# Routing in two batches, scaled expert results in a table read linearly, and the bias product last, in a graph layer with a 16-expert block on one Trainium2 core

## The chip, the cores and the metric

The kernel runs on one core of one Trainium2 chip. Its time is device microseconds for one launch, as the median of several runs. TensorE is called PE in the profile, VectorE DVE, ScalarE ACT, GpSimd POOL and SyncE SP.

## The reference

There are 1250 nodes of 512 features and 20000 edges with a source, a destination, one of 4 types and a weight. Everything is float32.

```
xn  = layernorm(x)
msg = sum over types r of (xn[src] @ W_rel[r] + b_rel[r]) * (weight where type == r)
agg = segment_sum(msg, dst) / max(segment_sum(weight, dst), 1)
x1  = layernorm(xn + xn @ W_self + b_self + agg) * g1 + b1
y   = layernorm(x1 + gelu(x1 @ W_ffn1 + b_ffn1) @ W_ffn2 + b_ffn2) * g2 + b2
x   = x + y
xm  = layernorm(x)
p   = softmax(xm @ router_w.T + router_b)            # 16 experts
out = x + sum over the two experts e with the largest p of
          p[e] * (gelu(xm @ w1[e].T + b1[e]) @ w2[e].T + b2[e])
```

## The kernel before, in words

The nodes are padded to 1280, ten tiles of 128 rows. All stages are in one program; the engines meet by semaphores, and the order of the work on each engine is the order in which `program` writes it down.

**Products.** PE turns each normed tile (`turn_xn`, L749, three tiles ahead of the products) and multiplies it with the four type matrices and with W_self (`product`, L756). DVE writes the low parts of the turned tiles (`x_low`, L1051), takes the products out and adds biases (L1130), and works out the tables of the edges (`edge_tables`, L1077) after the third product. SP stores the results as a table of messages.

**Gathers and the first half.** POOL gathers 157 chunks of 128 message rows with indirect DMAs (L522). PE sums them in windows (`window_sums`, L787). ACT copies each window sum twice, plain and rounded (`sums_out`, L605), DVE subtracts (`low_sums`, L1154), and PE adds the windows to blocks (`add_windows`, L799). Beside this, for pairs of tiles `p`, PE does the two-layer product (`hidden`, `second`), DVE the norm before it (`first_norm`) and the two after it (`other_norms`, L1205), and PE turns the normed tile (`turn_xm`) and makes its 16 logits (`logits`). Both products of the routing wait for the last pair. When the last window is summed, POOL clears a tile of zeros (L527), and SP fills `xslot` and the end of `yslot` with it (L425).

**Routing.** With all logits there, DVE adds the router's bias, ACT takes the exponential, and DVE finds for all ten tiles at once the two experts of every node, its gates, and the row that it gets in `xslot`, where each expert's rows are put together and rounded up to tiles of 128 (L1303 to L1347). POOL then writes every tile twice with 20 indirect DMAs (L543), one for the first and one for the second expert. Meanwhile DVE makes the table of which expert a slot tile has (L1349 to L1363), and PE multiplies the gates with the experts' second biases (L930 to L941), which DVE adds to `x_res` (L1367).

**Experts.** SP loads slot tiles, five ahead, and PE handles 28 of them in a fixed order. In step `t` it turns the rows of tile t+2 (`turn_rows`, L949), does the first product of t+1, the second product of t, and turns the hidden rows of t+1 (`expert_tiles`, L985). DVE copies the hidden rows (L1374) and the result (`take`, L1376). SP stores the result as soon as `take` is done and then loads tile t+5 into the place of tile t's rows (L440 to L452). POOL loads the next expert's weights, one megabyte, when a place of the five is free (L549 to L558).

**End.** When all results are stored, POOL gathers for each node tile the two result rows (L569, 20 indirect DMAs), DVE scales and adds them to `x_res` (L1407, L1410), and SP stores the tile (L468).

## Time and profile before

| what | value |
|---|---|
| median of 3 runs | 641.01 us (640.02 to 641.83) |
| profiled execution, its own time | 639.41 us |
| its span, first to last instruction | 637.5 us |
| mean granted clock of PE | 0.905 of full speed |
| PE, DVE, ACT, POOL busy | 526.0, 320.0, 119.3, 229.9 us |
| experts, from the first turn of slot rows to the last `take` | 467.0 to 597.6 us |

The busy times are sums over the whole span and overlap. PE is busy for 82% of the span, but not evenly: it is nearly full up to 407 us and in the expert loop, and has little or nothing to do between 407 and 467 us and after 597 us.

### The profile page before, as it was taken

The numbers are of one execution on the slowest core, as the hardware profiler recorded it, in microseconds if no ns is written. First come the engines' busy times: TensorE is split into PE (matmuls) and PEld (weight loads), VectorE is DVE, ScalarE is ACT, GpSimd is POOL, SyncE is SP. The second block draws the span as 40 slices with busy tenths as digits, with TensorE's granted clock in tenths as the row PEclk, the third lists the DMA queues.
The fourth block names the chain that finished last, engine by engine and source line by source line (L and its number), as shares of the span: only waits on it lengthen the run. The fifth ranks groups of instructions, "written<-read, shape, count | busy, mean of one in ns | idle before, by whom it ended". The sixth has DMA issues, their size and how long they took to land.

```text
span 637.5 us, 7136 instructions
## 1 busy us (share of the span) xinstructions
PE 526.0 (82%) x2292; PEld 353.1 (55%) x2292; DVE 320.0 (50%) x847; ACT 119.3 (19%) x251; POOL 229.9 (36%) x270
## 2 busy tenths in 40 slices
PE   1999999999965999999999999529359999999300
PEld 1888888887612756656657667223146666666200
DVE  6788563212226145986977995948102222222144
ACT  2121101000111322322223312011022222222000
POOL 3630000037777777777773000004700011110273
PEclk9999999989977999999999999855569999999855
DMA  8427242249898677776774592442534477872285
GB/s 318 185 83 255 113 166 92 90 121 290 278 398 283 195 203 201 200 199 178 200 204 123 201 407 86 155 178 99 207 105 165 164 265 265 293 267 100 85 257 203
DMA packets 47703, 125.54 MB, mean 197 GB/s; under 512 B 6496, under 2 KB 7136, under 8 KB 45360
## 3 DMA queue, kind: packets, MB, share of 16 engines
q0 software_dynamic: 17344, 63.20, 32.3%
q1 hardware_dynamic: 27360, 57.57, 24.1%
q10 hardware_dynamic: 2960, 4.27, 2.3%
q8 instruction: 22, 0.36, 0.2%
q14 instruction: 17, 0.14, 0.1%
HBM read 85.70 MB, written 39.32 MB: 196 GB/s over the span
## 4 chain that ended last, share of the span: by engine, by line
PE 74%; POOL 8%; DVE 7%; issue 5%; DMA 4%; ACT 1%; POOLq 1%; ACTq 0%; SPq 0%; DVEq 0%
PE ps L828 11%; PE ps L839 10%; PE ps L961 8%; PE ps L978 8%; PE ps L762 7%; PE ps L763 7%; PE ps L764 7%; PE ps L794 6%; POOL greg L569 3%; POOL xslot L543 3%; PE ps L954 2%; POOL greg L522 2%; PE ps L805 2%; PE ps L860 1%; DMA x_res<-x 1%
## 5 line engine op out<-in xcount | busy, mean ns | idle before, releaser
L522 POOL DMA_INDIRECT greg<-msg,row_i x157 | 156.7, 998 | 145.0 <-DMA msg<-greg 93.6
L762 PE MATMUL ps<-w_hi,xT_hi 128*128 128x512 f32 x200 | 81.1, 405 | 0.0
L763 PE MATMUL ps<-w_lo,xT_hi 128*128 128x512 f32 x200 | 79.8, 399 | 0.0
L764 PE MATMUL ps<-w_hi,xT_lo 128*128 128x512 f32 x200 | 79.7, 398 | 0.0
L828 PE MATMUL ps<-freg,wreg 128*128 128x256 f32 x320 | 71.7, 383 | 0.8 <-ACT freg L622 0.8
L839 PE MATMUL ps<-wreg,freg 128*128 128x512 f32 x160 | 72.1, 598 | 0.0
L828 PEld LDWEIGHTS ps<-freg,wreg 128*128 128x128 f32 x320 | 60.3, 191 | 16.4 <-issue 7.5
L961 PE MATMUL ps<-wreg,freg 128*128 x224 | 55.7, 393 | 0.0
L978 PE MATMUL ps<-wreg,freg 128*128 x112 | 52.7, 593 | 0.9 <-ACT freg L709 0.9
L794 PE MATMUL ps<-greg,sel 128*32 128x512 f32 x320 | 47.9, 638 | 6.3 <-DMA greg<-msg,row_i 6.3
L543 POOL DMA_INDIRECT xslot<-work,pos_i x20 | 19.7, 986 | 85.2 <-DVE pos_i L1347 79.4
L1374 DVE COPY freg<-ps 128x256 f32<-128x256 f32 x28 | 11.9, 425 | 74.8 <-PE ps L961 74.8
L839 PEld LDWEIGHTS ps<-wreg,freg 128*128 128x128 f32 x160 | 29.3, 190 | 35.4 <-issue 35.3
L1130 DVE TENSOR_TENSOR greg<-ps,greg 128x512 f32<-128x512 f32 x40 | 27.5, 688 | 36.0 <-PE ps L764 36.0
L961 PEld LDWEIGHTS ps<-wreg,freg 128*128 128x128 f32 x224 | 42.2, 199 | 5.5 <-issue 0.4
L762 PEld LDWEIGHTS ps<-w_hi,xT_hi 128*128 128x128 f32 x200 | 38.0, 190 | 10.5 <-issue 1.7
L764 PEld LDWEIGHTS ps<-w_hi,xT_lo 128*128 128x128 f32 x200 | 38.1, 191 | 9.5
L763 PEld LDWEIGHTS ps<-w_lo,xT_hi 128*128 128x128 f32 x200 | 38.2, 191 | 8.8
L1157 DVE TENSOR_TENSOR q_lo<-q_all,q_hi 128x512 fp32r<-128x512 f32 x20 | 13.9, 694 | 54.2 <-ACT q_hi L610 53.5
L1378 DVE COPY greg<-ps 128x512 f32<-128x512 f32 x28 | 19.4, 692 | 38.5 <-PE ps L978 38.5
L954 PE MATMUL ps<-ident,greg 128*128 128x128 f32 x112 | 18.3, 291 | 22.0 <-DMA greg<-xslot 14.7
L608 ACT COPY q_all<-ps 128x512 f32<-128x512 f32 x20 | 11.7, 586 | 119.9 <-PE ps L794 119.9
(170 smaller groups left out, 648.3 us busy)
## 6 DMA issues: line engine op xcount, KB each, us to landing
wreg<-experts POOLq DMA_DIRECT2D x11, 1025.0 KB, 6.3
msg<-greg SPq DMA_DIRECT2D x40, 256.0 KB, 2.0
xslot<-greg SPq DMA_DIRECT2D x1, 8960.0 KB, 25.6
greg<-xslot SPq DMA_DIRECT2D x28, 256.0 KB, 4.1
yslot<-greg SPq DMA_DIRECT2D x28, 256.0 KB, 2.9
wreg<-experts SPq DMA_DIRECT2D x5, 1025.0 KB, 9.6
wreg<-w SPq DMA_DIRECT2D x8, 512.0 KB, 12.7
w_in<-w_rel ACTq DMA_DIRECT2D x3, 1024.0 KB, 6.5
```

Source lines behind the costliest of these rows:

```text
L522: nc.gpsimd.indirect_dma_start(gath[:, c % RING, :], None, msg, bass.IndirectOffsetOnAxis(ap=row_i[:, c:c + 1], axis=0)).then_inc(s_gath[c ...
L543: nc.gpsimd.indirect_dma_start(xslot, bass.IndirectOffsetOnAxis(ap=pos_i[:, 2 * t + c:2 * t + c + 1], axis=0), work[:, t, :], None).then_i ...
L762: nc.tensor.matmul(bank(t % 5), xT_hi[:, at], w_hi[:, i, wk], start=(k == 0), stop=False)
L763: nc.tensor.matmul(bank(t % 5), xT_hi[:, at], w_lo[:, i, wk], start=False, stop=False)
L764: mm = nc.tensor.matmul(bank(t % 5), xT_lo[:, at], w_hi[:, i, wk], start=False, stop=(k == KD - 1))
L794: mm = nc.tensor.matmul(ps[WIN * j:WIN * (j + 1), B_Q * D:(B_Q + 1) * D], sel[:, c, :], gath[:, at % RING, :], start=(i == 0), stop=(i == ...
L828: mm = nc.tensor.matmul(bank(B_F1 + (f + 1) % 2, 0, 2 * P), w1_v[:, k, f * P:(f + 1) * P], x1T[:, k, :, :].rearrange("p s n -> p (s n)"), ...
L839: mm = nc.tensor.matmul(bank(B_F2), hT[:, f, s * P:(s + 1) * P], w2_v[:, f, :], start=(f == 0), stop=(f == KF - 1))
L954: tr = nc.tensor.transpose(bank(m, k * P, P), xs[:, u % MR, k * P:(k + 1) * P], ident[:, :])
L961: mm = nc.tensor.matmul(bank(3, 0, EF), xsT[:, SCR[u % MR], k, :], wreg[:, ds(at + k * EF, EF)], start=(k == 0), stop=(k == KD - 1))
L978: mm = nc.tensor.matmul(bank(5 + m), ehT[:, m, f, :], wreg[:, ds(at + (KD * EF + f * D), D)], start=(f == 0), stop=(f == KE - 1))
L1130: v.tensor_tensor(stage[:, n % 5, :], bank(t % 5), bias[:, V_REL + r, :], ALU.add).then_inc(s_evac, 1)
```

## The change

- The transposes of the first stage run two tiles ahead of the products, not three. The plain copy `q_all` is gone: DVE subtracts from PSUM itself. POOL adds the second norm's bias to `x_res` early, so `other_norms` has one DVE operation less.
- Routing is done in two batches, tiles 0 to 7 and tiles 8 and 9, by two new DVE functions, `choose` (experts) and `place` (rows). Batch 0's parts stand before and after the norms of tile 8, and POOL scatters its 16 times while DVE goes on. Batch 1's rows go into what is left of the tiles, or behind them, so the rows of a slot tile may lie in two stretches.
- Rows of `xslot` are 516 words wide: features, twice the node's number, its first expert, and its two gates. The slots are cleared after the last gather is issued; a second DMA then writes the number of each slot into one column.
- POOL loads each slot tile by an indirect gather, four ahead, and writes each result, scaled with its gate by DVE, with an indirect scatter to `results[2 * node + which]`. SP loads the experts' weights.
- At the end SP loads `results` linearly, a pair of tiles per DMA, and DVE adds without scaling. The product of gates and second biases is done after the expert loop.

The diff, cut to its core:

```diff
+BATCHES = ((0, NT - 2), (NT - 2, NT))
+AHEAD = 4
+BIAS_TILES = ((0, 4), (4, 8), (8, NT))
...
@@ SP @@
+            def clear_slots(before):
+                sp.dma_start(slots, empty_slots.unsqueeze(1).to_broadcast([P, SLOT_TILES, XW])).then_inc(s_zero, 16)
+                sp.wait_ge(s_zero, before + 16)
+                sp.dma_start(slots[:, :, C_ID:C_ID + 1], slot_ids.unsqueeze(2),
+                             allow_slow_non_contiguous=True).then_inc(s_zero, 16)
...
-            sp.wait_ge(d_sc, 16 * 2 * NT)
-            for u in range(MR):
-                load_x(u, u)
-            with sp.Fori(0, LOOPED - 1) as it:
-                for u in range(MR):
-                    store(it * MR + u, u)
-                    load_x(it * MR + (u + MR), u)
+            sp.wait_ge(d_tab, 1)
+            for e in range(EXPERTS):
+                if e >= MR:
+                    sp.wait_ge(e_y, done[e - MR])
+                    load_expert(sp, e)
+                sp.wait_ge(e_w[e % MR], 16 * (e // MR + 1))
+                sp.sem_inc(e_landed, 1)
+            results_out(0, USUAL)
+            for p in range(PAIRS):
+                sp.dma_start(both[:, 2 * p:2 * p + 2, :],
+                             results[4 * p * P:4 * (p + 1) * P, :].rearrange("(t p c) d -> p t (c d)", t=2, c=2))\
+                    .then_inc(f_in[p], 16)
@@ POOL @@
+            def scatter(r, b):
+                pool.wait_ge(r.pos, b + 1)
+                for t in range(*BATCHES[b]):
+                    for c in range(2):
+                        nc.gpsimd.indirect_dma_start(
+                            xslot, bass.IndirectOffsetOnAxis(ap=pos_i[:, c, t:t + 1], axis=0),
+                            rows_w[:, t, :], None).then_inc(r.sc, 16)
+            pool.wait_ge(s_zero, 32)
+            for b in range(len(BATCHES)):
+                scatter(r_fast, b)
...
+            def rows_to_tile(t):
+                if t >= MR:
+                    pool.wait_ge(e_xT, t - MR + 1)
+                    pool.wait_ge(e_prep, 2 * (t - MR + 1))
+                nc.gpsimd.indirect_dma_start(
+                    xs[:, t % MR, :], None, xslot,
+                    bass.IndirectOffsetOnAxis(ap=trow_i[:, t:t + 1], axis=0)).then_inc(e_x[t % MR], 16)
+            def tile_to_results(t):
+                pool.wait_ge(e_yt, t + 1)
+                nc.gpsimd.indirect_dma_start(
+                    results, bass.IndirectOffsetOnAxis(ap=node_i[:, t % MR:t % MR + 1], axis=0),
+                    ys[:, t % MR, :], None).then_inc(e_out[t % MR], 16)
+            def expert_tiles(first, end):
+                for t in range(first, min(first + AHEAD, end)):
+                    rows_to_tile(t)
+                for t in range(first, end):
+                    tile_to_results(t)
+                    if t + AHEAD < end:
+                        rows_to_tile(t + AHEAD)
+            pool.wait_ge(r_fast.sc, 2 * NT * 16)
+            pool.wait_ge(d_rows, 1)
+            expert_tiles(0, USUAL)
@@ PE @@
-            for t in range(3):
+            for t in range(2):
                 turn_xn(t)
...
+                if p == PAIRS - 1:
+                    second(fast, p, 1, 0, 6)
+                    counts(r_fast, 0)
+                    second(fast, p, 1, 6, 8)
...
...
             with pe.If(tiles_used(pe) > USUAL):
                 expert_begin(USUAL)
                 expert_rest(USUAL, SLOT_TILES)
+            expert_biases()
@@ DVE @@
+            choose(r_fast, fast, cs, 0)
             other_norms(fast, cs, NT - 2)
+            place(r_fast, cs, 0)
             other_norms(fast, cs, NT - 1)
+            choose(r_fast, fast, cs, 1)
+            place(r_fast, cs, 1)
...
             def low_sums(s):
-                v.tensor_tensor(q_lo[:, s % 2, :], q_all[:, :], q_hi[:, s % 2, :], ALU.subtract).then_inc(s_qlo, 1)
+                v.tensor_tensor(q_lo[:, s % 2, :], bank(B_Q), q_hi[:, s % 2, :], ALU.subtract).then_inc(s_qlo, 1)
...
+            def of_tile(to, row):
+                did(v.tensor_tensor(tval, tcmp, row.unsqueeze(1).to_broadcast(tab), ALU.mult))
+                did(v.tensor_reduce(to, tval, AX.X, ALU.add))
+            did(v.tensor_tensor(tcmp, tbase.unsqueeze(2).to_broadcast(tab), end_now.unsqueeze(1).to_broadcast(tab), ALU.is_ge))
+            rd.did(v.tensor_reduce(texp, tcmp, AX.X, ALU.add))
+            of_tile(tstart, room_now)
+            of_tile(tfrom, room_old)
+            of_tile(told, change_old)
...
+            v.tensor_tensor(trow_i[:, :], tpos, tstart, ALU.add).then_inc(d_rows, 1)
...
+            def take(it, u):
+                t = it * MR + u
                 dve.wait_ge(e_y, t + 2)
-                v.tensor_copy(ys[:, u, :], bank(5 + SCR[u])).then_inc(e_yt, 1)
+                dve.wait_ge(e_prep, it * (2 * MR) + 2 * (u + 1))
+                v.tensor_scalar(ys[:, u, :], bank(5 + SCR[u]), gate[:, u:u + 1], None, ALU.mult).then_inc(e_yt, 1)
...
             for t in range(NT):
-                dve.wait_ge(f_g[t % 4], 32 * (t // 4 + 1))
-                v.scalar_tensor_tensor(out=x_res[:, t, :], in0=yg[:, t % 4, 0, :], scalar=m8[:, t, 0:1],
-                                       in1=x_res[:, t, :], op0=ALU.mult, op1=ALU.add).then_inc(f_dve, 1)
+                dve.wait_ge(f_in[t // 2], 16)
+                v.tensor_tensor(x_res[:, t, :], x_res[:, t, :], both[:, t, 0:D], ALU.add).then_inc(f_dve, 1)
```

`choose` adds the router's bias, finds the eight largest of each node's 16 logits and their places, and makes two one-hot tables and their sum. `place` takes the counts that PE makes from that sum (`counts`), adds them up over the tiles, rounds them up to 128, and reduces ranks to row numbers. A new `gates_of` picks each slot row's gate and its row of `results`, four small DVE operations per slot tile.

## Rows read from the trace of the kernel before

**Rows 1.** The page, part 4: shares of the chain that ended last.

```profile
PE 74%; POOL 8%; DVE 7%; issue 5%; DMA 4%; ACT 1%; POOLq 1%; ACTq 0%; SPq 0%; DVEq 0%
```

**Rows 2.** Windows by stage: length, busy of each engine, PEclk, DMA share, GB/s.

```profile
407.00:467.00 60.00, 26.13 (x56) 12.01 (x56) 30.25 (x122) 5.32 (x15) 20.22 (x25) 0.53 0.46 184
467.00:597.00 130.00, 121.05 (x504) 83.40 (x504) 30.68 (x56) 33.09 (x85) 9.38 (x33) 0.97 0.58 197
597.00:637.50 40.50, 0.00 (x0) 0.00 (x0) 15.54 (x21) 0.00 (x0) 21.24 (x20) 0.55 0.63 201
```

**Rows 3.** Timeline of the first products: start, length, engine, line, operation.

```profile
15.56 0.78 PE L762 MATMUL ps<-w_hi,xT_hi 128*128 128x512 f32 x1
...
35.59 0.60 PE L753 MATMUL ps<-ident,work 128*128 128x128 f32 x4
...
38.83 0.60 PE L753 MATMUL ps<-ident,work 128*128 128x128 f32 x4
...
40.07 0.68 DVE L1054 TENSOR_TENSOR xT_lo<-ps,xT_hi 128x512 fp32r<-128x512 f32 x1
```

**Rows 4.** Timeline of the last norms and logits.

```profile
399.45 0.19 ACT L645 COPY lg<-ps 128x32 f32<-128x32 f32 x1 [1.10 <-PE ps L860]
...
408.03 0.69 DVE L1212 TENSOR_TENSOR freg<-freg,work 128x512 f32<-128x512 f32 x1
...
413.33 0.69 DVE L1218 TENSOR_TENSOR x_res<-x_res,freg 128x512 f32<-128x512 f32 x1
...
417.04 0.55 DVE L1221 TENSOR_SCALAR work<-x_res,mv,sm 128x512 f32<-128x512 f32 x1
...
423.07 0.19 ACT L645 COPY lg<-ps 128x32 f32<-128x32 f32 x1 [3.69 <-PE ps L860]
```

**Rows 5.** DVE's groups by line between 423 and 437 us: busy us, mean ns.

```profile
L1334 DVE TENSOR_TENSOR greg<-greg,ps 128x16 f32<-128x16 f32 x10 | 1.7, 170 | 0.3
...
L1350 DVE TENSOR_TENSOR freg<-num,row 1x576 f32<-1x576 f32 x1 | 0.7, 740 | 0.0
...
L1345 DVE TENSOR_TENSOR greg<-greg 128x160 f32<-128x160 f32 x2 | 0.6, 324 | 0.1
```

**Rows 6.** The page, part 6: the DMA that clears the slots, us to landing.

```profile
xslot<-greg SPq DMA_DIRECT2D x1, 8960.0 KB, 25.6
```

**Rows 7.** POOL's scatters, one line's view: ns min/median/max, first and last start, landing.

```profile
L543 POOL DMA_INDIRECT xslot<-work,pos_i x20: 967/971/1263, 437.1 to 461.6; - x20
...
DMA to landing us min/median/max: 2.7/2.7/3.0
```

**Rows 8.** PE's turns of slot rows, same view: 28 tiles of four.

```profile
L954 PE MATMUL ps<-ident,greg x112: 272/273/477, 467.0 to 586.3; 128*128 128x128 f32 x112
```

**Rows 9.** Timeline of the expert loop: turns of slot rows and takes.

```profile
480.83 0.60 PE L954 MATMUL ps<-ident,greg 128*128 128x128 f32 x4
...
503.37 0.69 DVE L1378 COPY greg<-ps 128x512 f32<-128x512 f32 x1 [1.25 <-PE ps L978]
...
507.43 0.60 PE L954 MATMUL ps<-ident,greg 128*128 128x128 f32 x4
...
511.58 0.69 DVE L1378 COPY greg<-ps 128x512 f32<-128x512 f32 x1 [1.36 <-PE ps L978]
```

**Rows 10.** Landing of POOL's message gathers (L522), all 157.

```profile
DMA to landing us min/median/max: 3.2/3.8/7.8
```

**Rows 11.** Landing of the slot tiles' linear loads (L439), 467 to 500, then 500 to 566 us.

```profile
DMA to landing us min/median/max: 2.6/2.8/7.0
...
DMA to landing us min/median/max: 3.1/4.2/6.3
```

**Rows 12.** PE's bias products, one line's view; two records per tile.

```profile
L940 PE MATMUL ps<-eb_s,freg x20: 1056/1056/1217, 434.9 to 451.2; 16*128 16x512 f32 x20
```

**Rows 13.** Timeline: the last take, and DVE's last operation.

```profile
596.90 0.69 DVE L1378 COPY greg<-ps 128x512 f32<-128x512 f32 x1 [2.42 <-PE ps L978]
...
633.19 0.75 DVE L1410 SCALAR_TENSOR_TENSOR x_res<-greg,m,x_res 128x512 f32<-128x512 f32 x1
```

More of the change, by code:

```diff
@@ new lines, in program @@
+        tval = room(TAB * EXPERTS).rearrange("p (t e) -> p t e", e=EXPERTS)
+        empty_slots = flat(tval)[:, 0:XW]
+        both = wreg[:, 0:2 * NT * D].rearrange("p (t n) -> p t n", t=NT)
+        tbase, texp, tstart, told, tfrom, tlater, tpos = (room(TAB) for _ in range(7))
+        tring = tfrom
+        slot_ids = tpos[:, 0:SLOT_TILES]
+        row16 = sb("row16", [P, 8, EXPERTS])
+        room_old, end_old, at_old, less, room_now, end_now, later_by, change_old = (row16[:, i, :] for i in range(8))
@@ L510, in _ @@
             nc.gpsimd.tensor_tensor(vec[:, V_F2 - V_G1, :], vec[:, V_F2 - V_G1, :], vec[:, V_B1 - V_G1, :], ALU.add).then_inc(s_sb, 1)
+            for t in range(NT):
+                pool.wait_ge(s_xn, t + 1)
+                nc.gpsimd.tensor_tensor(x_res[:, t, :], x_res[:, t, :], vec[:, V_B2 - V_G1, :], ALU.add).then_inc(s_xb, 1)
             pool.wait_ge(s_idx, 1)
@@ L606, in sums_out @@
                 act.wait_ge(s_q, s + 1)
-                after(act, s_qlo, s)
-                nc.scalar.copy(q_all[:, :], bank(B_Q)).then_inc(s_qc, 1)
                 after(act, s_l2, s - 1)
@@ L854, in turn_xm, with counts @@
                     tr.then_inc(c.xmT, 1)
+            def counts(r, b):
+                tiles = slice(*BATCHES[b])
+                n = EXPERTS * (tiles.stop - tiles.start)
+                at = 2 * EXPERTS * tiles.start
+                pe.wait_ge(s_qlo, STEPS)
+                pe.wait_ge(r.oh, b + 1)
+                after(pe, r.cntt, b)
+                nc.tensor.matmul(bank(B_Q, at, n), tri_bf[:, :], flat(oh_bf[:, tiles, :]), start=True, stop=True)
+                nc.tensor.matmul(bank(B_Q, at + n, n), ones_bf[:, :], flat(oh_bf[:, tiles, :]),
+                                 start=True, stop=True).then_inc(r.cnt, 1)
             def logits(c, p):
@@ L1173, in norm_stats @@
[L1173 to L1177 removed]
+                for s, r in enumerate(rows):
+                    n.did(v.bn_stats(st[:, s, :], r))
@@ new lines, in norm_stats @@
+                sync(n)
+                for s in range(k):
+                    n.did(v.bn_aggr(mv[:, s, :], st[:, s, :]))
+                sync(n)
+                var2, seed, sq, root = nvar[:, 0:k], nseed[:, 0:k], nsq[:, 0:k], nrs[:, 0:k]
+                did(v.tensor_scalar(var2, mv[:, 0:k, 1], EPS, None, ALU.add))
+                n.did(v.tensor_scalar(seed.bitcast(I32), var2.bitcast(I32), 1, None, ALU.logical_shift_right))
+                if k == 1:
+                    n.did(v.tensor_scalar(newton[:, :], nscale[:, :], var2, None, ALU.mult))
@@ new lines, in choose @@
+                did(v.tensor_tensor(lg[:, tiles, 0:EXPERTS], lg[:, tiles, 0:EXPERTS],
+                                    rb_s[:, :].unsqueeze(1).to_broadcast([P, k, EXPERTS]), ALU.add))
+                for t in range(a, z):
+                    n.did(v.max(lg[:, t, EXPERTS:], lg[:, t, 0:EXPERTS]))
+                sync(n)
+                v.tensor_tensor(low[:, tiles, :], lg[:, tiles, :],
+                                lg[:, tiles, EXPERTS:EXPERTS + 1].to_broadcast([P, k, EXPERTS + 8]),
+                                ALU.subtract).then_inc(r.low, 1)
@@ new lines, in choose @@
+                for t in range(a, z):
+                    n.did(v.max_index(i8[:, t, :], lg[:, t, EXPERTS:], lg[:, t, 0:EXPERTS]))
+                sync(n)
+                for c_ in range(2):
+                    n.did(v.tensor_copy(idx_f[:, c_, tiles], i8[:, tiles, c_]))
+                sync(n)
+                for c_ in range(2):
+                    n.did(v.tensor_tensor(choice[:, c_, tiles, :], num[:, 0:EXPERTS].unsqueeze(1).to_broadcast([P, k, EXPERTS]),
+                                          idx_f[:, c_, tiles].unsqueeze(2).to_broadcast([P, k, EXPERTS]), ALU.is_equal))
@@ L1286, in _ @@
                 for t in range(NT):
+                    zs.did(v.tensor_tensor(x_res[:, t, :], x_res[:, t, :], vec[:, V_B2 - V_G1, :], ALU.add))
+                sync(zs)
+                for t in range(NT):
                     after(dve, slow.x1T, t - 3)
@@ L1293, in _ @@
                         other_norms(slow, zs, t)
-                dve.wait_ge(slow.lgt, PAIRS)
+                dve.wait_ge(s_zero, 64)
+                for b in range(len(BATCHES)):
+                    choose(r_slow, slow, zs, b)
+                    place(r_slow, zs, b)
             rd = Steps(d_dve)
```

548 lines of the change are left out of this document (304 added, 244 removed).

## The prediction, made before the changed kernel was run

> **What bounds the kernel now.** I read the chain of waits first, then the busy time by stage, then the timeline of the stages that the change touches. The chain is three quarters PE [rows 1], so what counts is when PE has work. The stages show two places where it has little: 407 to 467 us, where it is busy 26 of 60 us at a granted clock of 0.53, and after 597 us, where it does nothing for 40.5 us [rows 2]. Between them stands the expert loop, where PE is busy for 121 of 130 us. The first hole is a chain: norm of tile 9, its logits, DVE's routing, 20 scatters, the load of the first slot tile. The last is POOL's 20 gathers with DVE behind. The change attacks both holes, and it touches the full stage between them: it puts POOL's indirect DMAs into the loop's supply.
>
> **First products: nothing.** With one turn fewer ahead, the first product needs no third transpose. It starts at 15.6 us now [rows 3] and could start when DVE's first low part is there, at about 13.7 (an estimate: that is before the three-tile group's norm, and the four transposes and their wait go). That is 1.9 us. But DVE waits for the turn of tile 7 before it begins the tables of the edges, and that turn now comes one product later: turns are 3.24 us apart (35.59 to 38.83) [rows 3]. So the tables come 3.24 - 1.9 = 1.3 us later, and the low part behind them, now 40.07 to 40.75, ends near 42.1. The product that needs it starts at about 42.0 today (38.83, the four transposes, then one product of 2.8). I take 0, bounds -1.9 and +0.5. `q_all`'s copy leaves one ACT copy out of the chain to the first norm: -0.5, bounds -1 and 0; elsewhere PE already waits for the same subtraction before it adds windows, so the new wait costs nothing. POOL's ten adds on `x_res` lie before its gathers, when it is idle.
>
> **Routing: -16.** Batch 0's `choose` can begin when the fourth pair's logits are there, at 399.64 [rows 4]. For eight tiles it is 6 wide operations of 0.3 us (324 ns for 160 columns [rows 5]), 8 maxima and 8 index searches, some 2 us together, and two small copies: 4.0 us, to 403.6. The norms of a tile take 408.03 to 417.59, 9.56 us [rows 4], less the add that goes (0.72 with its gap): 8.8. Tile 8 is done at 412.4. `place` for batch 0 has eight dependent adds of 0.2, some eight wide operations of 0.3 and eight small ones of 0.17: 5.6 us, to 418.0. Tile 9's norms end at 426.8, against 417.6 now: this is what batch 0 costs the chain, 9.2 us. From the end of the norms to the copied logits is 5.7 us today (417.59 to 423.26 [rows 4]), so 432.5. For two tiles `choose` is 2.0 and `place` 4.0: 438.5, against 436.8 today. So DVE has the last rows 1.7 us later than now; the gain is behind it. POOL issues a scatter every 1.29 us (20 from 437.1 to 461.6 [rows 7]): the 16 of batch 0 run 418.3 to 439.0, hidden by the norms, and only 4 are left, to 444.1, landed by 445.6. DVE's table of rows is longer: tcmp, texp and three pairs of 576 elements, eight operations of 0.74 [rows 5] with gaps 6.2 us, and a dozen small ones, 2.2: 446.9, so DVE is last, by 1.3. A gather of tile 0 from 447.2 with 3.6 us to land gives 450.8, and PE turns it at 451.0 against 467.0 [rows 8]. **-16.0**, bounds -18 and -13. Had batch 0's scatters no cover they would cost their 20.7 us. ACT's early load of the Gelu table I count as nothing: PE reads its own tables at that point. The clear takes 25.6 us [rows 6] and now starts near 344, when the last gather is issued, and ends near 370; the column of 4480 single words has no row here; it has until 418.
>
> **Expert loop: +23.** This is the term that decides. Count the lead of a load. In step t PE does the second product of t, and `take(t)` follows. PE turns tile t+4 one whole step later: a take starts at 503.37 and the turn at 507.43, **4.06 us** [rows 9]. Today the load of t+4 left a step earlier and through SP, with eight us of lead. In the changed kernel POOL first waits for `take(t)`, scatters its result, and only then gathers t+4. After the start of the take come: the take itself 0.69 [rows 9], DVE to POOL 0.3 (an estimate from the gap before the first scatter), the scatter's slot 1.29 [rows 7], so the gather starts **2.3 us** behind the take's start and must land within 1.8. No gather of this trace did: 3.2 us is the shortest of 157 and 3.8 the median [rows 10]. So PE waits in every step. From turn t+4 to `take(t+2)` is 4.15 us (507.43 to 511.58), so turns obey: turn(t+4) is no earlier than turn(t+2) + 4.15 + 2.35 + g, with g the landing time. That binds pairs: two steps take 6.5 + g. At g = 4.2 a step is 5.35 us, against 4.11.
> Turn 3 is at 480.83 [rows 9] and turn 27 at 586.1 [rows 8]: 24 steps in 105.3 us, 98.6 of them at 4.11 and the rest five breaks in which PE reads its tables; a break runs beside the wait, so it is hidden up to the wait's length. With the rule, 12 pairs: 12 x (6.5 + g) - 105.3, which is +11 at g = 3.2 (+13 with what of the breaks is not hidden), +18 at 3.8, **+23** at 4.2, +29 at 4.7.
> Which g? In the quiet first part a linear load lands in 2.8 us, in the busy part, with the experts' megabytes beside it, in 4.2: the neighbours add 1.4 us [rows 11]. POOL's gathers begin at 3.2 to 3.6, the busy part is half of the loop, so 3.2 plus 0.3 to 1.4: I take 4.2, near what the same loop's loads need in their busy part, between 3.2 and 4.7. What DVE gets extra, four small operations of some 0.17 per tile, fits between its take and the next hidden copy. POOL's two slots, 2.6 us, fit into a step.
>
> **End: -0.5.** Today the last take ends at 597.59 and DVE's last operation at 633.94 [rows 13]: 36.4 us. Afterwards the gates' table takes DVE 1 us, and ten transposes with three copies 2.5, so bias products begin near 601. A tile of them took 1.71 us in the stretch where they now lie (ten tiles, 434.9 to 452.3 [rows 12]); PE stood at its lower level then, 1.2 GHz, and 17 us of such products without a gap did not lift it (the whole stretch reads 0.53 [rows 2]). I take the lower level again, since PE is idle before them: 618.3, and the last add at 619. The linear loads are 5.2 MB from about 602; at the 201 GB/s of this stage [rows 2] they are in by 628, and the last pair is needed at 630.5. 20 adds of 0.72 (a take's 0.69 and a gap) make 14.4: 633.4. -0.5, bounds -9 (2.4 GHz) and +3 (late loads).
>
> **Sum.** 0 - 0.5 - 16.0 + 23 - 0.5 = **+6** on a span of 637.5 and a time of 639.41 for the profiled execution; that execution is 1.6 below the median of the runs, 641.01, and I put the difference on the median: **647 us**.
>
> **Rivals.**
> *Quick gathers, faster than before.* With only four or five DMAs in flight a gather could land in 2.7 to 3.4, as the scatters did (2.7, at most 3.0 [rows 7]). It is the same mechanism with another price: +9 in the loop at 2.7 (the unhidden breaks included) and so 633; +13 at 3.2 and so 637. The change wins from g below about 3.6. For it: a step that is longer spreads the bytes. Against it: these are 128 rows of 2 KB read at random with a megabyte load beside them two steps in five, and the 157 gathers never did better than 3.2. The Trainium skill, "DMA: Bandwidth & Descriptors", section on the anatomy of one DMA, fits a POOL-issued transfer with 2.0 us plus its bytes at 436 GB/s, which for this size would be 2.6 us, an estimate after that page; by it the sum would be 632. This trace's gathers do not agree with it, at 3.2 and more, its scatters nearly do. Chance 0.24.
> *The bias products run at 2.4 GHz.* PE kept its clock in the first us after its last product; if it holds through transposes and products, these take 8.6 us and not 17.1, and the end becomes -9: 638.5. Against it is the long stretch at the low level [rows 12]. Chance 0.08, mostly faster.
> *The slots are not ready.* If the one-word column took over 48 us, POOL would start batch 0's scatters late, and every us beyond 418 would come back in full: 650 to 665. Chance 0.04.
> *PE's clock falls in the loop.* Waits of 1.2 us per step, longer beside a megabyte, could bring it to 1.2 GHz for parts: a turn's matmul took 477 ns against 272 then [rows 8]. Some 20 us more, 665. Chance 0.04.
>
> **How the numbers follow.** The forecast, PE waiting in each step with g from 3.6 to 5.2, has 0.60 and spans 641 to 657; 0.05 of it lies within 0.3% of no change (about what a measurement of this kernel can tell), 0.55 above. Of the quick gathers 0.22 is faster and 0.02 the same. Of the fast bias products 0.06 is faster, 0.01 the same, 0.01 slower. The two last are slower. Together faster 0.28, same 0.08, slower 0.64. The range reaches down to g = 2.7, 633, and up to g = 5.2, 657. The likeliest case alone is 641 to 657.
>
> **What would show it.** In the changed profile the first turn of slot rows should stand near 451, and batch 0's scatters at 418 to 439. In the loop PE should wait before the turns for POOL's gathers, 24 times, 20 us and more in all, with a gather's start 2.3 us behind each take and turns 5.3 apart. After the loop there should be 17 us of bias products at a clock of 0.5. I am wrong if gathers land in under 3.4 us, if PE does not wait at its turns, or if the first turn comes after 455.

## The result, and the profile after

| | before | after |
|---|---|---|
| median of 4 runs each | 640.51 us (639.59 to 641.83) | 657.51 us (654.26 to 659.00) |
| ratio | | 1.0257, 95% interval 1.0214 to 1.0300 |
| profiled execution, its own time | 639.41 us | 657.54 us |
| its span | 637.5 us | 655.7 us |

The changed kernel is slower by 17.0 us, 18.2 in the two spans. The page's chain of waits, part 4, shares of the span:

```profile
PE 58%; issue 15%; DVE 12%; POOL 8%; DMA 4%; ACT 1%; DVEq 0%; SPq 0%; POOLq 0%; ACTq 0%
```

TensorE had three quarters of the chain before [rows 1] and has 58% now: time has gone to whatever TensorE waits for. The windows of the changed kernel, cut at the first logits' addition, at the first turn of slot rows and behind the last take, show where (columns as in [rows 2]):

```profile
402.00:458.00 56.00, 13.99 (x52) 8.77 (x52) 38.69 (x181) 5.50 (x10) 22.73 (x23) 0.60 0.51 195
458.00:618.60 160.60, 129.58 (x504) 85.98 (x504) 44.95 (x168) 33.32 (x84) 50.90 (x52) 0.94 0.49 161
618.60:655.70 37.10, 18.69 (x30) 7.29 (x30) 20.82 (x34) 1.31 (x3) 1.03 (x1) 0.53 0.57 219
```

The middle row is the expert loop. It held 121 us of TensorE work in 130 before [rows 2]. Now it has 129.6 in 160.6, and its share of DMA has gone down from 0.58 to 0.49: it starves. Set against the kernel before, by stations:

| station | before | after | difference |
|---|---|---|---|
| logits of the fourth pair there, first addition possible | 399.64 | 403.10 | +3.5 |
| first turn of slot rows | 467.03 | 457.88 | -9.2 |
| end of the last take | 597.59 | 618.65 | +21.1 |
| end of the span | 637.5 | 655.7 | +18.2 |

So routing gave 9.2 us at the first turn, less than the 16 forecast; the loop took 30.2 more (160.77 us against 130.56); and what follows the last take became 2.9 us shorter (37.05 against 39.91).

**The loop.** TensorE's transposes of slot rows in part 5 of the page, then the landing of the loop's 28 gathers (L596) between 500 and 575 us and between 575 and 620 us:

```profile
L1030 PE MATMUL ps<-ident,greg 128*128 128x128 f32 x112 | 19.3, 298 | 49.0 <-DMA greg<-xslot,trow_i 45.5
```
```profile
DMA to landing us min/median/max: 3.2/4.5/8.0
```
```profile
DMA to landing us min/median/max: 3.2/3.3/3.5
```

Of the 45.5 us, 20.1 are the wait before the first turn. The other 25.4 are waits inside the loop, at 20 of the 27 later turns. The gathers land much like the linear loads they replace, 3.1/4.2/6.3 in the same busy part [rows 11]. What changed is when they start, as one step of the timeline shows:

```profile
476.55 0.75 DVE L1558 TENSOR_SCALAR greg<-ps,gate 128x512 f32<-128x512 f32 x1 [1.29 <-PE ps L1054]
477.58 1.00 POOL L602 DMA_INDIRECT results<-greg,node_i  x1 [1.83 <-DVE greg L1558]
478.89 0.96 POOL L596 DMA_INDIRECT greg<-xslot,trow_i  x1 [0.30 <-PE ps L1030]
...
484.50 0.80 PE L1030 MATMUL ps<-ident,greg 128*128 128x128 f32 x3 [1.94 <-DMA greg<-xslot,trow_i]
```

A take at 476.55, its scatter at 477.58, the gather behind it at 478.89, 2.34 us after the take's start, and TensorE at 484.50, having waited 1.94. The 2.3 us stand in 23 of the 24 steps that have a gather.

**Ahead of the routing.** DVE's low parts of the first products, and the TensorE row that waits for one:

```profile
36.25 0.69 DVE L1131 TENSOR_TENSOR xT_lo<-ps,xT_hi 128x512 fp32r<-128x512 f32 x1 [1.95 <-ACT xT_hi L632]
37.45 0.23 DVE L1157 TENSOR_SCALAR greg<-greg 128x160 f32<-128x160 int32 x1
...
42.70 0.68 DVE L1131 TENSOR_TENSOR xT_lo<-ps,xT_hi 128x512 fp32r<-128x512 f32 x1
...
44.13 0.59 PE L825 MATMUL ps<-w_hi,xT_hi 128*128 128x512 f32 x1 [2.07 <-DVE greg L1207]
```

The edge tables begin at 37.45, and the low part behind them is 2.63 us later than its 40.07 [rows 3]. They begin when DVE has the low part of tile 7, and so behind that tile's turn. Before and after:

```profile
32.35 0.60 PE L753 MATMUL ps<-ident,work 128*128 128x128 f32 x4
```
```profile
35.00 0.60 PE L816 MATMUL ps<-ident,rows_w 128*128 128x128 f32 x4
```

The turn comes 2.65 us later, although the first product starts 2.03 us earlier, at 13.53 against 15.56.

**The tables.** DVE's last positions and the first operation of the tables:

```profile
440.98 0.17 DVE L1399 CAST pos_i<-placef 128x4 int32<-128x4 f32 x1
...
445.21 0.18 DVE L1498 TENSOR_TENSOR row<-row 128x15 f32<-128x15 f32 x1 [4.06 <-issue]
```

Between them DVE does nothing for 4.06 us, and "issue" says that it waited for nothing that the profile shows. In the source, the branch on the general path stands there, with the load of its flag into a register. In the kernel before it stood ahead of a wait for the logits.

**The end.** After the last take:

```profile
621.77 17.43 PE L1018 MATMUL ps<-eb_s,freg 16*128 16x512 f32 x20 [0.75 <-ACT freg L750]
622.58 2.67 SPq L495 DMA_DIRECT2D wreg<-results  x5
623.88 0.69 DVE L1594 TENSOR_TENSOR x_res<-x_res,ps 128x512 f32<-128x512 f32 x1 [4.17 <-PE ps L1018]
...
639.24 0.69 DVE L1594 TENSOR_TENSOR x_res<-x_res,ps 128x512 f32<-128x512 f32 x1 [1.02 <-PE ps L1018]
639.96 0.69 DVE L1598 TENSOR_TENSOR x_res<-x_res,wreg 128x512 f32<-128x512 f32 x1
```

The bias products take the 17 us foreseen, at the lower clock (the window reads 0.53), and DVE never waits for the linear loads.

### The profile page after: what moved, and what is told of

Same layout as the page of the kernel before. It is cut to its first block, busy times and chain, and to the rows that moved or that the text cites. A ratio compares the mean times of both kernels' runs of the same rounds, so it can differ in the third digit from the quotient of the medians.

```text
span 655.7 us, 7222 instructions
## 1 busy us (share of the span) xinstructions
PE 535.3 (82%) x2294; PEld 359.1 (55%) x2294; DVE 342.5 (52%) x997; ACT 110.4 (17%) x226; POOL 266.9 (41%) x281
## 4 chain that ended last, share of the span: by engine, by line
PE 58%; issue 15%; DVE 12%; POOL 8%; DMA 4%; ACT 1%; DVEq 0%; SPq 0%; POOLq 0%; ACTq 0%
PE ps L891 11%; PE ps L902 10%; PE ps L825 7%; PE ps L826 6%; PE ps L827 6%; PE ps L857 6%; POOL results L602 3%; POOL greg L596 3%; PE ps L1018 3%; DMA greg<-xslot,trow_i 2%; PE ps L934 2%; PE ps L1037 2%; PE ps L868 1%; PE ps L870 1%; PE ps L1054 1%
## 5 line engine op out<-in xcount | busy, mean ns | idle before, releaser
L557 POOL DMA_INDIRECT greg<-msg,row_i x157 | 153.5, 978 | 132.6 <-DMA msg<-greg 79.2
L825 PE MATMUL ps<-w_hi,xT_hi 128*128 128x512 f32 x200 | 82.8, 414 | 6.7 <-issue 4.0
L826 PE MATMUL ps<-w_lo,xT_hi 128*128 128x512 f32 x200 | 81.3, 406 | 0.0
L602 POOL DMA_INDIRECT results<-greg,node_i x28 | 27.9, 996 | 102.4 <-DVE greg L1558 98.0
L1037 PE MATMUL ps<-wreg,freg 128*128 x224 | 59.5, 413 | 0.0
L1030 PE MATMUL ps<-ident,greg 128*128 128x128 f32 x112 | 19.3, 298 | 49.0 <-DMA greg<-xslot,trow_i 45.5
L1054 PE MATMUL ps<-wreg,freg 128*128 x112 | 54.6, 610 | 0.9 <-ACT freg L766 0.9
L565 POOL DMA_INDIRECT xslot<-rows_w,pos_i x20 | 19.8, 991 | 80.1 <-DVE pos_i L1399 74.3
L857 PE MATMUL ps<-greg,sel 128*32 128x512 f32 x320 | 45.0, 627 | 6.7 <-DMA greg<-msg,row_i 6.2
L902 PEld LDWEIGHTS ps<-wreg,freg 128*128 128x128 f32 x160 | 29.2, 190 | 34.9 <-issue 34.8
L1037 PEld LDWEIGHTS ps<-wreg,freg 128*128 128x128 f32 x224 | 44.2, 208 | 5.9
L1030 PEld LDWEIGHTS ps<-ident,greg 128*128 128x128 f32 x112 | 12.7, 147 | 54.4 <-DMA greg<-xslot,trow_i 50.5
L1558 DVE TENSOR_SCALAR greg<-ps,gate 128x512 f32<-128x512 f32 x28 | 21.0, 751 | 38.6 <-PE ps L1054 38.6
```

Of the source, the lines that this page charges most:

```text
L557: nc.gpsimd.indirect_dma_start(gath[:, c % RING, :], None, msg, bass.IndirectOffsetOnAxis(ap=row_i[:, c:c + 1], axis=0)).then_inc(s_gath[c ...
L602: nc.gpsimd.indirect_dma_start(results, bass.IndirectOffsetOnAxis(ap=node_i[:, t % MR:t % MR + 1], axis=0), ys[:, t % MR, :], None).then_i ...
L825: nc.tensor.matmul(bank(t % 5), xT_hi[:, at], w_hi[:, i, wk], start=(k == 0), stop=False)
L826: nc.tensor.matmul(bank(t % 5), xT_hi[:, at], w_lo[:, i, wk], start=False, stop=False)
L857: mm = nc.tensor.matmul(ps[WIN * j:WIN * (j + 1), B_Q * D:(B_Q + 1) * D], sel[:, c, :], gath[:, at % RING, :], start=(i == 0), stop=(i == ...
L902: mm = nc.tensor.matmul(bank(B_F2), hT[:, f, s * P:(s + 1) * P], w2_v[:, f, :], start=(f == 0), stop=(f == KF - 1))
```

## The experiments

**The order on GpSimd in the loop.** Two runs ask what paces the loop.

```diff
 for t in range(first, end):
-    tile_to_results(t)
     if t + AHEAD < end:
         rows_to_tile(t + AHEAD)
+    tile_to_results(t)
```

> Edit: on GpSimd the gather of tile t+4 is issued ahead of the scatter of tile t, instead of behind it. Theory A (the loop is paced by one cycle: take of a result, scatter issue 1.3 us, gather issue 1.3 us, landing, turn of the tile four ahead, so the gather starts about 2.3 us behind the take's start and has 4.06 us of room): each gather now starts a step of 4 us earlier, TensorE's waits for gathers (42 records, 45.5 us on PE) nearly vanish, the loop from the first turn to the end of the last take falls from 160.8 us to 131 to 135, and the time to 629 to 633. Theory B (the loop's added time is the cost of indirect transfers as such, in DMA contention, in 2064 B rows, or in VectorE's four added instructions a tile): the waits shrink little, the loop stays above 150 us, the time above 645.

Measured: 632.62 us (630.15 to 634.06), 24.9 less than the changed kernel and 0.9857 of the kernel before (0.9818 to 0.9895). The loop is 136.6 us, a little above the 131 to 135 of theory A. TensorE's row in part 5, and two steps of the timeline:

```profile
L1030 PE MATMUL ps<-ident,greg 128*128 128x128 f32 x112 | 18.2, 287 | 30.9 <-DMA greg<-xslot,trow_i 23.7
```
```profile
500.62 0.75 DVE L1558 TENSOR_SCALAR greg<-ps,gate 128x512 f32<-128x512 f32 x1 [1.29 <-PE ps L1054]
...
502.95 0.96 POOL L596 DMA_INDIRECT greg<-xslot,trow_i  x1 [0.30 <-issue]
...
504.72 0.75 DVE L1558 TENSOR_SCALAR greg<-ps,gate 128x512 f32<-128x512 f32 x1 [1.30 <-PE ps L1054]
```

The waits inside the loop fall from 25.4 to 3.5 us. The gather of t+4 still starts 2.3 us behind a take, but it is the take of the tile before t: 1.77 us ahead of its own, so the lead has grown by a whole step. All 28 gathers, 28 scatters, the rows of 2064 bytes and DVE's four operations a tile are unchanged, and they cost at most the 6 us that are left. The gathers land in 3.3/4.0/7.9 us (shortest, median, longest), no faster than the 3.2/3.7/8.0 of the changed kernel. Theory A holds, theory B falls.

The other direction, `AHEAD = 3`:

> Edit: AHEAD = 3 instead of 4, the order on GpSimd as it was. Theory A: every tile, not one in two or three, waits for its gather: a step is the whole cycle of about 6.5 us plus a landing of 3.7 to 4.2 us, 10.2 to 10.7 us, less the part of a step by which a turn stands ahead of its product, so 30 tiles take 200 to 320 us and the time rises by 50 us or more. Theory B: the number of tiles ahead is no limit; the time rises by less than 10 us.

Measured: 831.13 us, 173.6 more (one run). The loop is 334.4 us, with 11.1 to 13.8 us from take to take:

```profile
L1030 PE MATMUL ps<-ident,greg 128*128 128x128 f32 x112 | 31.2, 434 | 174.7 <-DMA greg<-xslot,trow_i 172.8
```

Nearly every tile now waits 5.4 to 7.1 us, against landings of 3.2/3.4/4.9 us, shorter than in the changed kernel. Theory A holds in kind, but a step and the loop are longer than the 10.7 and 320 us it allowed. Part of that is the clock: a transpose takes 434 ns in the mean, against 298, 460 to 790 us run at a granted clock of 0.77, and TensorE is busy for 174.7 us there, against 129.6 in the loop of the changed kernel. So the same gathers make TensorE wait 3.5 us in the loop, 25.4 or over 150, by the step in which they are issued.

**The first 60 us.** Two suspects: the transposes two ahead, and GpSimd's ten additions to `x_res`.

```diff
-            for t in range(2):
+            for t in range(3):
                 turn_xn(t)
...
-                if t + 2 < NT:
-                    turn_xn(t + 2)
+                if t + 3 < NT:
+                    turn_xn(t + 3)
```

> Edit: the transposes of the first products stand three tiles ahead again (as before the change), nothing else. Theory A (the late start of the low parts, found in two waits of TensorE for xT_lo of 0.6 and 2.3 us, is the loss of the first part): TensorE's 2.3 us wait at 41.5 to 44.1 us goes, and all that follows, the window sums (195.5 us) among it, comes 2 to 3 us earlier. Theory B (the loss of 4.8 us up to the window sums comes from the ten added additions on GpSimd, 44.6 to 60.6 us, beside which VectorE's one-hot instructions take 0.90 and 1.40 us instead of 0.42 and 0.43): the first product starts later, near 15.6 us, and the window sums start at 194 to 196 us as now.

And the additions held back behind DVE's one-hots:

```diff
+            pool.wait_ge(s_prod, 4 + STEPS + 3)
             for t in range(NT):
                 pool.wait_ge(s_xn, t + 1)
                 nc.gpsimd.tensor_tensor(x_res[:, t, :], x_res[:, t, :], vec[:, V_B2 - V_G1, :], ALU.add)
```

> Edit: GpSimd waits for product 27 (after the last one-hots of VectorE) before its ten additions to x_res; transposes two ahead as in the changed kernel. Theory B (contention with the ten additions): VectorE's one-hots take 0.42 and 0.43 us again, the steps of products 5 to 12 fall from 2.87 us to 1.39, and the window sums come 3 to 4 us earlier, at 191.5 to 192.5 us, the time falls by as much. Theory A (the two-ahead transposes are the loss): the one-hots may be quicker but the window sums come less than 1.5 us earlier.

And the transposes two ahead in the kernel before, the mirror of the first:

> Edit: the kernel before, with the transposes of the first products two tiles ahead instead of three, nothing else. Theory A (VectorE's additions of products 0 to 4 stand behind low parts whose transposes now come one product later, so the edge tables and the low part of tile 8 come later, and TensorE waits): the first product starts 1.5 to 2 us earlier, yet the first gather comes 2 to 3.5 us later than its 135.65, and the time rises by as much, to 642 to 644. Theory B (the loss belongs to other work of the changed kernel, as the ten additions on GpSimd): the first gather comes at 133.5 to 136 us.

The first gather of messages, which waits for all products, is the mark. In the order kernel before, kernel before with two ahead, changed kernel, three ahead, additions later:

```profile
135.65 1.18 POOL L522 DMA_INDIRECT greg<-msg,row_i  x1 [93.59 <-DMA msg<-greg]
```
```profile
138.02 1.18 POOL L522 DMA_INDIRECT greg<-msg,row_i  x1 [93.15 <-DMA msg<-greg]
```
```profile
139.87 1.17 POOL L557 DMA_INDIRECT greg<-msg,row_i  x1 [79.23 <-DMA msg<-greg]
```
```profile
137.18 1.17 POOL L557 DMA_INDIRECT greg<-msg,row_i  x1 [79.22 <-DMA msg<-greg]
```
```profile
138.89 1.17 POOL L558 DMA_INDIRECT greg<-msg,row_i  x1 [25.63 <-DMA msg<-greg]
```

Theory A holds in all three runs, that the transposes are the larger loss. Of the 4.2 us, 2.7 go with the two-ahead transposes (2.4 when they are put into the kernel before alone) and 1.0 with the additions. How sure is that? In five profiles in which this part is the same code (the changed kernel, the order swapped, `AHEAD = 3`, and two runs that follow) the mark lies between 139.48 and 140.47. So the transposes stand clear of the spread, and the 1.0 is no more than its width, though 138.89 lies below all five. Four later profiles with both edits put it at 135.84 to 136.73, so together they give back nearly all. The transposes are the larger part in both kernels: DVE evacuates product n only behind the low part of tile n+5, whose transposes come one product later. The times say less than the marks. The two edits of the changed kernel took 651.73 and 657.01 us, one run each, and its loop, untouched by them, came out between 157.2 and 163.5 us from run to run. The edit of the kernel before took 641.71 us (one run), where 642 to 644 were expected and the unedited kernel took 638.81 to 642.24 beside it.

The additions do more to DVE than the mark shows. Its groups from 45 to 60 us, in the changed kernel and with the additions later (busy us, mean ns, idle before):

```profile
L1190 DVE TENSOR_TENSOR sel<-sel,w_e 128x256 f32<-128x256 f32 x4 | 5.6, 1397 | 0.1
L1187 DVE TENSOR_TENSOR sel<-num,greg 128x256 f32<-128x256 f32 x4 | 3.8, 950 | 0.0
L1207 DVE TENSOR_TENSOR greg<-ps,greg 128x512 f32<-128x512 f32 x5 | 3.4, 678 | 0.0
L1196 DVE TENSOR_TENSOR w_lo<-w_in,w_hi 128x2048 fp32r<-128x2048 f32 x1 | 3.4, 3379 | 0.0
```
```profile
L1208 DVE TENSOR_TENSOR greg<-ps,greg 128x512 f32<-128x512 f32 x8 | 5.5, 684 | 0.0
L1197 DVE TENSOR_TENSOR w_lo<-w_in,w_hi 128x2048 fp32r<-128x2048 f32 x2 | 4.6, 2292 | 1.5 <-ACT w_hi L650 1.5
L1191 DVE TENSOR_TENSOR sel<-sel,w_e 128x256 f32<-128x256 f32 x6 | 2.6, 425 | 0.2
L1188 DVE TENSOR_TENSOR sel<-num,greg 128x256 f32<-128x256 f32 x6 | 2.5, 417 | 0.0
```

Beside the additions a one-hot's second operation takes 1397 ns instead of 425 and the weights' low part 3379 instead of 2292, while the evacuation, whose first operand is in PSUM, keeps its 0.68 us (678 ns against 684). The Trainium skill, "GPSIMD Engine Reference", section Specifications, names such contention for DVE instructions with two SBUF inputs; by that rule it is the one-hots and the low part that must suffer and the evacuation that must not, and these rows agree. Over all twenty one-hots and three low parts between 40 and 100 us DVE is busy 7.6 us longer (12.4, 10.9 and 8.0 us against 8.5, 8.3 and 6.9), yet only 1 us of that reaches the mark.

**The 4 us at the tables.**

```diff
+            wanted = general_wanted(dve)
             choose(r_fast, fast, cs, 1)
             place(r_fast, cs, 1)
 
-            with dve.If(general_wanted(dve)):
+            with dve.If(wanted):
```

> Edit: VectorE loads the flag of the general path into its register before the wait for the last logits, and not between the second batch's positions and the tables. Theory A (the 4.06 us in which VectorE ran nothing there, 441.16 to 445.21, is the register load with its latency): the gap falls below 1.5 us, the first gather and the first turn of the loop come 2.5 to 4 us earlier against the first logits' addition. Theory B (it is the branch itself, or code that has to be fetched for what follows): the gap stays over 3 us and the first turn where it is.

Measured: 652.65 us (one run), and the gap is 3.31 us, not 4.06:

```profile
440.65 0.17 DVE L1399 CAST pos_i<-placef 128x4 int32<-128x4 f32 x1
444.13 0.18 DVE L1499 TENSOR_TENSOR row<-row 128x15 f32<-128x15 f32 x1 [3.31 <-issue]
```

Theory A falls: most of the gap stays. The load is worth less than the pair 4.06 and 3.31 says, since the same gap in five other profiles with the load in its old place reads 4.02, 4.04, 3.76, 3.76 and 3.60 us, and 3.31 again in a later one with the load early. So the load is 0.3 to 0.75 us, and 3.3 stay with the branch. Then the branch itself was moved, on the kernel with four edits below, ahead of the second batch's choice, where DVE waits for the logits anyway:

> Edit, on the kernel with the four edits: VectorE's branch on the general path stands ahead of the second batch's choice, where VectorE waits 5.7 us for the last logits, with the choice and the placing of the second batch in both arms. Theory A (the 3.3 us left between the last positions and the tables are the branch itself, and a wait of 5.7 us can hide it): that gap falls below 0.5 us, the first turn comes about 3 us earlier, and the time is 620 to 622 us against 623.9. Theory B (what costs is the start of code that has not run yet, wherever it stands): the same 3 us appear at the head of the second batch's choice or of the tables, and the first turn stays.

Measured: 620.2 us (one run), the first turn at 451.63 against 455.36. The wait for the logits is as long as ever, and the tables follow the positions at once:

```profile
433.42 0.19 DVE L1327 TENSOR_TENSOR lg<-lg,rb_s 128x32 f32<-128x32 f32 x1 [5.69 <-ACT lg L689]
...
438.88 0.17 DVE L1400 CAST pos_i<-placef 128x4 int32<-128x4 f32 x1
438.96 0.17 DVE L1503 TENSOR_TENSOR row<-row 128x15 f32<-128x15 f32 x1
```

Theory A holds: the first turn is 3.7 us earlier, of which 0.3 stem from the logits, and the 3.3 us vanish in a wait of 5.7. The Trainium skill, "Advanced Engine Details and Errata", section Control Flow Timing, puts a compare and branch at 108 ns, a figure that this case's row exceeds thirtyfold; here the branch also leaps over all the code of the general path. One trace of the leap is there: in the gap of the changed kernel the two DMA queues that the profile calls "instruction" move a block each, at 442 to 443 and 443 to 444 us, and in the kernel with the four edits likewise at 440 to 441 and 441 to 442, inside its gap. With the branch moved, the first of the two queues moves a block at 430 to 431 and one at 432 to 433, inside the wait. That fits a fetch of the code behind the leap, but the profile doesn't say for which engine a block is, and no run separates the branch from the fetch: which of them costs stays open.

**The end.** The bias products and their additions left out:

> Edit: the twenty bias products and their ten additions at the end are left out (so the output lacks the experts' second bias). Theory A (the bias products at TensorE's low clock, 17.4 us from 621.77, set the end of the changed kernel): the first of the last 20 additions starts at the landing of the first linear load, 5 to 9 us after the last take instead of 21.3, and what follows the last take falls from 37.0 us to 21 to 25. Theory B (the five linear loads of 1 MB bound the end, landing 9.3 us in the median): the additions wait for the loads and the end comes no more than 6 us earlier.

Measured: 650.13 us (one run). What follows the last take is 26.8 us instead of 37.0:

```profile
630.45 0.69 DVE L1592 TENSOR_TENSOR x_res<-x_res,wreg 128x512 f32<-128x512 f32 x1 [7.91 <-DMA wreg<-results]
```

The first addition comes 9.0 us after the last take, as theory A had it, but the end takes 26.8 us and not its 21 to 25. Both bounds are there, one behind the other: without the bias DVE waits 7.9 us for the first linear load, and later 0.65 and 1.2 for two more. So the bias products at the end are worth 10 us and not their 17.4.

**Together.** The gather first, three transposes ahead, the additions later and the flag early:

> Edit: the gather ahead of the scatter in the loop, the transposes three ahead, GpSimd's ten additions behind product 27, and VectorE's flag loaded early, together, on the changed kernel. Theory A (four separate losses on one path): they add up, 24.9 (measured), 2.7 (measured), 1.0 (measured) and up to 4, so 632.6 falls to 624 to 629 us, below the kernel before by 2 to 2.5 per cent. Theory B (they overlap, since one wait hides another, for instance the scatters' landing or the clear of the slots behind the flag): 629 to 633 us.

Measured: 623.88 us (621.64 to 625.97), ratio to the kernel before 0.9731 (0.9689 to 0.9772). That is 33.6 us less than the changed kernel, and at the edge of theory A. The losses did not hide one another, but they don't add up to it either: 24.9, 2.7, 1.0 and the 0.75 of the flag make 29.4. Against the profile with the order alone swapped, the first turn comes 3.2 us earlier, which the three other edits cover, the loop is 3.4 shorter and the end 1.7. None of the three lies in the loop or the end. 1.8 us of the loop are one stretch at the lower clock that the other profile has, where a turn and its take are 5.91 us apart and not 4.1; the rest stays open. The loop is 133.2 us against 130.56 before the change, so of its 30.2 lost us 27.5 are back.

On top of it the bias products ahead of the loop. In short:

```diff
+            pe.wait_ge(d_gall, 1)
+            gates_turned(0)
+            gates_turned(1)
...
+            for t in range(3):
+                expert_bias(t)
             turn_xm(fast, PAIRS - 1)
             logits(fast, PAIRS - 1)
             counts(r_fast, 1)
...
+            expert_bias(3)
...
-            expert_biases()
```

> Edit, on the kernel with the four edits: the bias products stand ahead of the loop (tiles 0 to 2 ahead of the last norm's transposes, 3 to 9 behind the second batch's counts), their additions beside the tables; the general path, which these inputs do not take, is left without them. Theory A (at the end they stand alone, 17.4 us at TensorE's low clock, where the linear loads would be through after 8 us; ahead of the loop they run in TensorE's idle time): the stretch behind the last take falls from 35.5 us to 25 to 27, the first turn comes 0 to 4 us later, and the time falls by 5 to 10 us, to 614 to 619. Theory B (ahead of the loop they delay the last logits, the tables and the first turn by what they save): the time stays within 3 us of 623.9.

Measured: 615.69 us (one run). 26.6 us follow the last take, and the first turn comes at 456.65, 1.3 later than with the four edits:

```profile
439.17 6.17 PE L996 MATMUL ps<-eb_s,freg 16*128 16x512 f32 x7
445.28 0.59 PE L992 MATMUL ps<-ident,freg 128*16 128x128 f32 x2
446.32 3.78 PE L996 MATMUL ps<-eb_s,freg 16*128 16x512 f32 x4 [0.45 <-ACT freg L733]
456.65 1.09 PE L1053 MATMUL ps<-ident,greg 128*128 128x128 f32 x4 [6.56 <-DMA greg<-xslot,trow_i]
```

The products end at 450.1 and TensorE waits another 6.56 us for the gather: they fit in its idle time, and theory A holds in all three of its numbers. The price is that this kernel and the next leave the bias out on the general path, so their times stand for inputs like these alone. Last, all of it with the branch in the wait as well:

> Edit: the four edits, the branch in the wait for the logits, and the bias products ahead of the loop, together. If the parts add up, 623.9 less 3 less 5 to 10: 611 to 617 us, 4 to 4.5 per cent below the kernel before. If the additions of the bias, which now stand between the tables and the loop, eat what the branch gives, 614 to 620.

Measured: 616.19 us in the median of six runs (613.06 to 620.79), ratio 0.9633 (0.9595 to 0.9672). The profiled execution has its first turn at 452.77, 3.9 earlier than without the branch's move, but a loop of 133.2 us against 130.6 and the same 26.9 behind it. Against the kernel with the four edits the bias and the branch together give 7.7 us. What the branch's move adds in this pair isn't separable: the single 615.69 stands inside the range of the six runs.

## Why the prediction was right and where it was not

It said slower, by PE waiting in the loop for POOL's gathers, with 647 us; the time was 657.5, just above the range that ended at 657. The way and the mechanism of the loop were right. What failed were three terms: the size of the loop's, "first products: nothing", and DVE's path behind the last positions, in which the branch was missing. On the spans, +6 was forecast and +18.2 came: 7.4 of the 12.2 us between them lie ahead of the first turn, 7.2 in the loop, and -2.4 at the end. Step by step:

- **The mechanism of the loop: right, and shown.** The lead of 4.06 us, the gather 2.3 us behind the take's start (2.33 measured), the wait in front of the turns, at 20 of them where 24 were forecast. With a step more of lead the waits fall from 25.4 to 3.5 us, with a step less they grow to over 150.
- **The size of the loop: short by 7.** The term "two steps take 6.5 + g, at g = 4.2" gave +23 and measured +30.2, of which 29.4 lie between turn 3 and turn 27. These take 134.6 us, as if g were 134.6 / 12 - 6.5 = 4.7, the value that the prediction had at +29. Followed from gather to gather along the odd tiles, what is above 12 x (6.5 + 4.2) = 128.4 has three parts. The twelve gathers on this chain took 4.4 us from their start to the turn in the mean, not 4.2, and that by a single one:

```profile
547.78 0.96 POOL L596 DMA_INDIRECT greg<-xslot,trow_i  x1 [0.30 <-issue]
...
555.83 0.66 PE L1030 MATMUL ps<-ident,greg 128*128 128x128 f32 x4 [1.54 <-DMA greg<-xslot,trow_i]
```

  Its 8.0 us make up for the 3.3 to 3.6 of the last ones and 2.3 us more. Another gather, at 563.15, left 3.1 us behind its take and not 2.3, since its scatter waited for DVE's row numbers: 0.7 us. The largest part is the clock, at 3.4 us. Twice on this chain it fell, and there a turn and its take are 5.8 us apart instead of 4.1 (484.50 to 490.32, 507.39 to 513.22). A third such stretch, 548.27 to 554.11, lies on the even tiles, while the odd ones waited for the gather of 8.0 us. The windows of the two, and of a stretch beside:

```profile
477.00:482.00 5.00, 3.77 (x16) 2.72 (x17) 1.16 (x6) 1.08 (x3) 1.97 (x2) 1.00 0.89 275
484.50:489.50 5.00, 5.00 (x15) 3.85 (x16) 0.42 (x1) 0.58 (x1) 0.96 (x1) 0.66 0.34 109
507.40:512.40 5.00, 5.00 (x15) 3.58 (x16) 0.42 (x1) 0.59 (x1) 0.37 (x1) 0.66 0.75 296
```

  The column before the last two is the granted clock, 0.66 of 2.4 GHz in the mean of 5 us, so most of it at 1.2. The three stretches each followed a wait for a gather, of 1.94, 2.73 and 2.64 us. The prediction had this as a rival of its own with 0.04 and 20 us; it came along with the forecast's waits, at a sixth of that price.
- **Ahead of the first turn, -16.5 with the copy's -0.5: measured -9.2.** Two steps failed. The first is "the first products: nothing", a 0 with a bound of +0.5: it measured +3.5 at the first logits, of which 2.7 are the transposes. The sum had the pieces: tables 3.24 us later for a later turn, 1.9 earlier for the earlier first product, so 1.3. The earlier start came (2.03). But from there to the next turn it takes 4.47 us, against 3.82 before, and TensorE then waits 0.55 us, at 28.85, for the low part of tile 4, which DVE makes behind four norms that take it 5.11 us. So the tables come 2.64 us later and not 1.3, and the product behind them starts at 44.13 and not near 42. The same term had the ten additions "when it is idle": GpSimd was idle, but DVE beside it was not, and slowed. The second step is a term that was missing: the branch with its flag, 4.06 us, on DVE's path between positions and tables. The kernel before showed no such row, since DVE went from it into a wait; the listing of the code was the only place to see that the step had moved out of its cover. The 0.5 of the copy can't be seen: with transposes and additions back in place the last logits of batch 0 are still added 1.0 to 1.6 us later than 399.64. The rest of the path came 0.7 us better than forecast.
- **End, -0.5: measured -2.9.** Products of 17.4 us at the lower clock were right. The last twenty additions go at 0.67 us and not 0.72, and the outputs are out 2.4 us after the last one, against 3.6 before.
- **Its signs of being wrong.** One came: the first turn, at 457.88, is after its 455. Another was near: in the last part of the loop gathers landed in 3.2 to 3.5 us, about its 3.4, and TensorE waited all the same, by 0.2 to 1.0 us.
- **The slots not ready, the bias at 2.4 GHz.** Neither came: POOL's scatters waited for DVE's positions (74.3 of their 80.1 us of idle time before), and the bias ran at the lower clock.
- **Quick gathers, 0.24.** The fit in the Trainium skill, "DMA: Bandwidth & Descriptors", section on the anatomy of one DMA, which gave 2.6 us a gather as an estimate, does not fit these: none of the loop's 28 landed in under 3.2 us, in the changed kernel or with the order or the number ahead changed. By the prediction's own count the waits would not have gone even at 2.6, since 1.8 us is what the order left; no run had such gathers.

## What to carry to other kernels

When a transfer moves to another engine's queue, count its lead from the instruction that it now stands behind, not from its length: swapping two lines on GpSimd was worth 25 us, and the transfers became no faster. When work is moved out of a wait, list everything that the wait had covered, branches and register loads too, and put those where the next wait is. An addition given to an idle engine is free only if the busy one beside it keeps its durations, so compare those too.

## What the runs showed that was not expected

- A branch of DVE that leaps over a long path cost 3.3 us, and the register load in front of it 0.3 to 0.75; in a wait of 5.7 us both were free.
- DVE operations with both operands in SBUF took up to 3.3 times as long beside GpSimd's additions (1397 ns against 425); one with an operand in PSUM did not change (678 against 684).
- A loop whose loads come late can lose twice: after waits of 1.9 to 2.7 us TensorE's clock fell in three tiles in the middle of the loop, and with waits of 5.4 to 7.1 us in nearly every tile it stood at 0.77 in the mean and the loop took 334 us. Other waits of the same length, as one of 2.78 us, were not followed by a lower clock, and in the run with the order swapped it fell behind a break of 2.41 us in which PE waited for no gather (515.68 to 521.59, read at 0.71), so what decides stays open.
- 128 rows of 2 KB gathered through a table of rows landed nearly as fast as the same bytes loaded in a line, 4.5 us against 4.2 in the median beside the experts' loads.
